# A two-layer attention and expert kernel: rank-one updates added by DMA, experts split beside the first half

## The reference

```python
x = x + xattn(c, layernorm(x), ...)        # 8 heads of 128; keys and values from c and x together
x = x + ffn(layernorm(x), W1, W2, scale)   # hidden width 1024, with rank-one updates per batch
x = x + attention(layernorm(x), c, c)      # one head of width 256
x = x + experts(layernorm(x), ...)         # 8 experts of inner width 256, mixed by a routing weight
```

```python
lt = x[:, 1:17]                            # 16 rows of the normed batch
even, odd = lt[:, ::2], lt[:, 1::2]
m1 = (even[:, :4, :, None] * odd[:, :4, None, :]).reshape(B, 1024, 256)
m2 = (even[:, 4:, :, None] * odd[:, 4:, None, :]).reshape(B, 256, 1024)
h = gelu(x @ W1.T + scale * einsum('bsd,bhd->bsh', x, m1) + b1)
out = h @ W2.T + scale * einsum('bsh,boh->bso', h, m2) + b2
```

## Time and profile before

| | us |
|---|---|
| median of 3 runs | 1989.06 (1987.77 to 1990.6) |
| the profiled execution | 1991.09 |
| its span, first to last instruction | 1989.3 |
| TensorE, busy | 1927.2 (97%) |
| VectorE, busy | 1367.9 (69%) |
| ScalarE, busy | 1115.5 (56%) |
| GpSimd, busy | 407.1 (20%) |

### The profile page before, as it was taken

The page is one execution under the profiler, slowest core; times in us unless marked ns, Lnnn a source line. Parts: engine busy times, 40 slices in busy tenths (PEclk is TensorE's granted clock), DMA queues, the critical chain, the costliest instruction groups (busy, mean ns, idle before and its releaser), DMA issues.

```text
span 1989.3 us, 41475 instructions
## 1 busy us (share of the span) xinstructions
PE 1927.2 (97%) x14078; PEld 1803.2 (91%) x14078; DVE 1367.9 (69%) x3408; ACT 1115.5 (56%) x2334; POOL 407.1 (20%) x650
## 2 busy tenths in 40 slices
PE   7999999999999999999987899999999999999998
PEld 6788888888888888888886899999999999999998
DVE  7877776776777776776746566766666666766665
ACT  5655565555655565555655655554555555544553
POOL 2222222222222222222213511111111101111100
PEclk9999999999999999999999999999999999999999
DMA  4000000000000000000012200000000000000000
...
DMA packets 47211, 44.51 MB, mean 22 GB/s; under 512 B 6848, under 2 KB 45376, under 8 KB 47168
## 3 DMA queue, kind: packets, MB, share of 16 engines
...
## 4 chain that ended last, share of the span: by engine, by line
PE 83%; DVE 7%; ACT 5%; issue 3%; POOL 1%; SPq 1%; DMA 0%; DVEq 0%; ACTq 0%; POOLq 0%
PE ring L618 9%; PE ring L620 9%; PE ring L619 9%; PE ring L1820 7%; PE ring L1818 7%; PE ring L1819 7%; PE ring L671 4%; PE sim L1818 3%; PE sim L1819 3%; PE sim L1820 3%; PE sim L618 3%; PE sim L620 2%; PE sim L619 2%; PE ps_x L1818 2%; PE ps_x L1820 2%
## 5 line engine op out<-in xcount | busy, mean ns | idle before, releaser
L411 ACT ACTIVATE a_pr<-sim,a_nmax 128x512 f32<-128x512 f32 x256 | 174.5, 689 | 208.4 <-DVE a_nmax L537 208.3
L1818 PE MATMUL ring<-b_xch,b_weh 128*128 128x256 f32 x1024 | 289.5, 283 | 1.7 <-DVE b_act_e L1464 1.7
L1819 PE MATMUL ring<-b_xcl,b_weh 128*128 128x256 f32 x1024 | 285.7, 279 | 0.0
L1820 PE MATMUL ring<-b_xch,b_wel 128*128 128x256 f32 x1024 | 285.6, 279 | 0.0
L326 POOL TENSOR_SCALAR a_pr<-a_pr,a_rinv 128x512 f32<-128x512 f32 x256 | 183.1, 729 | 498.3 <-DVE a_rinv L547 495.4
L1818 PEld LDWEIGHTS ring<-b_xch,b_weh 128*128 128x128 f32 x1024 | 192.3, 188 | 1.9 <-DVE b_act_e L1464 1.9
L1819 PEld LDWEIGHTS ring<-b_xcl,b_weh 128*128 128x128 f32 x1024 | 193.0, 188 | 0.0
L1820 PEld LDWEIGHTS ring<-b_xch,b_wel 128*128 128x128 f32 x1024 | 192.1, 188 | 0.0
L1464 DVE TENSOR_TENSOR b_act_e<-b_act_e,ring 128x512 f32<-128x512 f32 x128 | 87.9, 687 | 116.7 <-PE ring L1820 102.4
L528 DVE TENSOR_TENSOR a_ptl<-ring,a_pth 128x512 fp32r<-128x512 f32 x256 | 163.9, 682 | 3.1 <-ACT a_pth L401 2.0
L515 DVE SCALAR_TENSOR_TENSOR a_ktl<-ring,a_bkv_s,a_kth 128x512 fp32r<-128x512 f32 x128 | 95.3, 744 | 102.1 <-ACT a_kth L391 102.1
...
## 6 DMA issues: line engine op xcount, KB each, us to landing
...
b_up<-b_ev SPq DMA_DIRECT2D x256, 1.0 KB
...
```

The costliest lines, as they stand in the source:

```text
L411: nc.scalar.activation(pr[:, h % 2, t, :], sim[t][:], ACT.Exp, bias=nmax[:, h % 2, t:t + 1], accum_out=rsum[:, h % 2, t:t + 1]).then_inc(e ...
L1818: nc.tensor.matmul(out, lh, rh, start=(n == 0), stop=False)
L1819: nc.tensor.matmul(out, lh, rl, start=False, stop=False)
L1820: last = nc.tensor.matmul(out, ll, rh, start=False, stop=(n == len(parts) - 1 and not more))
```

## The change

1. The rank-one updates are written into the weights. 8 ScalarE instructions of 128x256 for W1 and 8 for W2 (`update`; GpSimd does them for batches 0 and 1) write scale x even x odd into `w1_raw` and `w2_raw`. One DMA for each matrix (`weights_added`, from GpSimd's queue, with `accum_op=ADD`) adds W1 or W2 from DRAM to it. Then the sum is split again for each batch: 8 copies of 128x512 (`weight_high`) on ScalarE, 8 subtractions on VectorE (`weight_low`; GpSimd does most for batches 0 and 1).
2. The 16 rows are normalised apart: SyncE loads 32 rows of x1 two batches ahead (`rows_load`), `rows_stats`, `rows_rstd` and `rows_apply` norm them, `rows_in_order` turns those for W2, and SyncE writes them to DRAM (`rows_between`) and reads them back: the even ones broadcast to all partitions (`even_b`, 1 MB), the odd ones with one number per element (`odd_raw`, 2 loads); `odd_scaled` multiplies these by the scale.
3. `z_fill`, the `up1` matmul in `h_fill`, `g_fill`, `y_update` and what served them are gone, and `y_fill` has 256 columns. `bias_x1`, `bias_x2` and the row shifts move from GpSimd to VectorE. The chain's steps, routing and weights of experts stand in another order within the body; `third_residual` writes a buffer of its own, `x3_s`.
4. The experts' weights are split in batches 1 to 8 of the first half, one expert in each (`spare`): SyncE loads 768 KB, ScalarE makes three copies and VectorE three subtractions, and SyncE writes both halves to DRAM (`expert_halves`). `experts_in` loads both, 12.6 MB in all, and the second half splits no expert. Batch 0 no longer loads or splits W1 and W2.
5. Batch 14 of the first half (`ahead`) makes the weights of the second half's batch 0, and batch 15 (`beside`) those of batch 1. The first half's loop is now batch 0, 1 to 8, 9 to 13, 14, 15; the second half's is bodies 1 to 13, 14, 15, 16.

```diff
         body(sections["first"], 0, False, True)
-        with eng.Fori(1, B - 1) as b:
+        with eng.Fori(1, 1 + SPARE) as b:
+            body(Order(loop_names, loop_first - F, sections["first"], F, b), b, True, True, True)
+        with eng.Fori(1 + SPARE, B - 2) as b:
             body(Order(loop_names, loop_first - F, sections["first"], F, b), b, True, True)
+        body(Order(loop_names, tail_first - F, Order(loop_names, 0)), B - 2, True, True)
...
-        with eng.Fori(2, B - 1) as t:
-            body(t, True, True, False)
+        with eng.Fori(1, B - 2) as t:
+            body(t, True, True, True)
+        body(B - 2, True, True, False)
         body(B - 1, True, False, False)
         body(B, False, False, False)
...
-        def updates_of(n):
-            take(ev_lo, n + 1)
...
+        def rows_load(n):
+            sp.dma_start(first_rows[:], x1_r[n]).then_inc(rows_in, 16)
+        def rows_spread(n):
+            take(rows_ready, n + 1)
+            sp.dma_start(z_t[n, 0:2 * NL], first_rows[1:1 + 2 * NL, :]).then_inc(rows_out, 16)
+            sp.dma_start(z_two[n, 1, NL:2 * NL], first_rows[2 + 2 * NL:2 + 4 * NL:2, :]).then_inc(rows_out, 16)
+            take(rows_turned, n + 1)
+            sp.dma_start(z_two[n, 0, NL:2 * NL], turned_rows[1 + 2 * NL:1 + 4 * NL:2, :]).then_inc(rows_out, 16)
+            take(rows_out, n * 48 + 48)
+            if not (isinstance(n, int) and n == 0):
+                take(w_made["2"], n * 4)
+            sp.dma_start(even_b[:], z_two[n, 0].unsqueeze(0).to_broadcast([P, 2 * NL, D])).then_inc(spread_in, 16)
+            for c in range(DC):
+                sp.dma_start(odd_raw[:, c, :], z_two[n, 1][:, c * P:(c + 1) * P].rearrange("r p -> p r"),
+                             allow_slow_non_contiguous=True).then_inc(spread_in, 16)
...
-            for j, w in enumerate((Wg[e], Wu[e], Wd[e])):
-                sp.dma_start(we_raw[e][:, j], w.rearrange("(c p) d -> p c d", p=P)).then_inc(expert_in[e], 16)
+            for part, tile in enumerate((weh[e], wel[e])):
+                sp.dma_start(f32(tile[:]).rearrange("p j c d -> p (j c d)"), kept[part, e]).then_inc(expert_in[e], 16)
+        def spare(h, b):
+            if h == 0:
+                take(split_out, b * 32)
+                sp.dma_start(w1_raw[:].rearrange("p c n -> p (c n)")[:, 0:3 * DC * D], We[b - 1]).then_inc(split_in, 16)
+            else:
+                take(split_lo, b * 3)
+                for part, tile in enumerate((w1h, w1l)):
+                    sp.dma_start(kept[part, b - 1], all_thirds(tile)).then_inc(split_out, 16)
...
+        def odd_scaled(n):
+            take(spread_in, n * 48 + 48)
+            nc.gpsimd.tensor_scalar(odd[:], odd_raw[:], lscale, 1.0, ALU.mult, ALU.mult).then_inc(odd_ready, 1)
+            take(odd_ready, n + 1)
...
+        def update(n, w, q):
+            if n > 0:
+                take(full["H", 3] if w == "1" else y_full, n if w == "1" else n * ST)
+            for k in range(2):
+                part, row, by = rank_one(w, q, k)
+                last = nc.gpsimd.tensor_scalar(part, row, by, 1.0, ALU.mult, ALU.mult)
+            last.then_inc(w_made[w], 1)
...
+        def weights_added(n, w):
+            take(w_made[w], n * 4 + 4)
+            if w == "1":
+                dst, src = w1_raw[:].rearrange("p c n -> p (c n)"), W1T.rearrange("p c n -> p (c n)")
+            else:
+                dst, src = w2_raw[:], W2T.rearrange("p c d -> p (c d)")
+            pool.dma_start(dst, src, accum_op=ALU.add, max_dma_last_dim=HC * W2ROW * 2).then_inc(w_in[w], 16)
...
+        def update(n, w, q):
+            act.wait_ge(odd_ready, n + 1)
+            if w == "1":
+                act.wait_ge(full["H", 3], n)
+            else:
+                act.wait_ge(y_full, n * ST)
+            for k in range(2):
+                part, row, by = rank_one(w, q, k)
+                last = nc.scalar.activation(part, row, ACT.Copy, scale=by)
+            last.then_inc(w_made[w], 1)
+        def weight_high(n, w, q):
+            act.wait_ge(w_in[w], n * 16 + 16)
+            raw, high, _ = (w_piece(w, q, tile) for tile in W[w])
+            nc.scalar.activation(high, raw, ACT.Copy).then_inc(w_hi[w], 1)
...
+        def spare(h, b):
+            if h < 3:
+                act.wait_ge(split_in, b * 16)
+                nc.scalar.activation(third(w1h, h), third(w1_raw, h), ACT.Copy).then_inc(split_hi, 1)
...
                 silu(i, 1)
-                routing_exps(i)
                 hidden_high(i, 1)
                 if chain:
                     gelu_high(t, 0)
                     gelu_high(t, 1)
-                for e in warm_in(1) if warm else ():
-                    for j in range(3):
-                        expert_high(e, j)
                 if chain:
                     gelu_high(t, 2)
                     gelu_high(t, 3)
+                routing_exps(i)
 
                 silu(i, 2)
                 if chain:
                     context_high(t)
                 hidden_high(i, 2)
-                for e in warm_in(2) if warm else ():
-                    for j in range(3):
-                        expert_high(e, j)
-                if chain:
-                    for k in range(ST):
-                        g_high(t, k)
-                    gt_copy(t)
+                if more:
+                    for q in range(4):
+                        update(t + 1, "1", q)
 
                 silu(i, 3)
                 hidden_high(i, 3)
-                for e in warm_in(3) if warm else ():
-                    for j in range(3):
-                        expert_high(e, j)
+                if chain:
+                    copy_high(t, "V", hh[:, V, 0:S])
+                if more:
+                    update(t + 1, "2", 0)
+                if chain:
+                    copy_high(t, "B", xth[:])
+                if more:
+                    update(t + 1, "2", 1)
 
                 silu(i, 4)
-                if chain:
-                    copy_high(t, "B", xth[:])
-                    copy_high(t, "V", hh[:, V, 0:S])
                 hidden_high(i, 4)
-                for e in warm_in(4) if warm else ():
-                    for j in range(3):
-                        expert_high(e, j)
                 if chain:
                     queries_high(t)
-                    row_shift_sums(t)
+                if more:
+                    update(t + 1, "2", 2)
+                    update(t + 1, "2", 3)
 
                 silu(i, 5)
+                if chain:
+                    softmax_exps(t)
+                hidden_high(i, 5)
                 if more:
-                    even_high(t + 1)
-                hidden_high(i, 5)
-                if chain:
-                    softmax_exps(t)
+                    weight_high(t + 1, "1", 0)
+                    weight_high(t + 1, "1", 1)
+                if chain:
+                    copy_high(t, "T", hh[:, PT, 0:S])
                 silu(i, 6)
...
+        def weight_low(n, w, q):
+            dve.wait_ge(w_hi[w], n * 4 + q + 1)
+            raw, high, low = (w_piece(w, q, tile) for tile in W[w])
+            nc.vector.tensor_tensor(low, raw, f32(high), ALU.subtract).then_inc(w_lo[w], 1)
...
+        def row_shifts(n):
+            dve.wait_ge(ln_ready["B"], n + 1)
+            for k in range(ST):
+                last = nc.vector.scalar_tensor_tensor(pr[:, k, :], ln[:, k, :], 1.0, v_b[:], ALU.mult, ALU.mult,
+                                                      accum_out=row_sum[:, k:k + 1])
+            last.then_inc(shift_in, 1)
+            take(shift_in, n + 1)
+            nc.vector.tensor_scalar(row_shift[:], row_sum[:], shift[:, 0:1], None, ALU.add).then_inc(shift_ready, 1)
...
-        def z_fill(n):
-            pe.wait_ge(od_ready, n + 1)
-            for c in range(DC):
-                for k, x in enumerate((xth, xtl)):
-                    last = nc.tensor.matmul(bank(n, "Z")[:, 0:S], od[:, c, :], x[:, c, :],
-                                            start=(c == 0 and k == 0), stop=(c == DC - 1 and k == 1))
-            last.then_inc(full["Z"], 1)
...
         def h_fill(t, n):
             cd = halves(bank(t, ("H", n)))
             for k in range(2):
                 cols = slice((2 * n + k) * P, (2 * n + k + 1) * P)
-                product(cd[:, k, :], range(DC), lambda c: w1h[:, c, cols], lambda c: w1l[:, c, cols],
-                        lambda c: xth[:, c, :], lambda c: xtl[:, c, :], more=True)
-                last = nc.tensor.matmul(cd[:, k, :], up1[:, n, k * P:(k + 1) * P], zm[:], start=False, stop=True)
+                last = product(cd[:, k, :], range(DC), lambda c: w1h[:, c, cols], lambda c: w1l[:, c, cols],
+                               lambda c: xth[:, c, :], lambda c: xtl[:, c, :])
             last.then_inc(full["H", n], 1)
 
...
         def y_fill(t, k):
             q = slice(k * P, (k + 1) * P)
-            product(bank(t, f"Y{k}")[:, 0:W2ROW], range(HC), lambda c: hh[:, c, q], lambda c: hl[:, c, q],
```

(14 more changed lines are left out.)

676 lines of the change are left out of this document (345 added, 331 removed).

## The result

The changed kernel takes 1970.82 us (median of 4 runs, 1969.19 to 1973.13) against 1989.83: ratio 0.9907, 95% interval 0.9894 to 0.9920. The profiled execution has a span of 1969.4 us. It is faster, as forecast, but by 19 us instead of 60, and the time lies 1 us above the stated range.

The account below looks back on a forecast made before the run. TensorE, busy 97% of the span and holding 83% of the chain, was taken as the bound. Terms summed to 60.4 us off the profiled 1991.1, giving 1930.7, and 1929 us for the median; range 1914 to 1970.

Parts of the forecast that it names:

- steady bodies, t = 2 to 15: Second half's 14 steady bodies: 2.7 us saved less 0.3 of new waits, 2.4 us each, 33.6 us in all.
- the second half's first body: No expert is split there, so it falls from 67.28 to 53.7 us: 13.6 us gained, bounds 10 to 14.
- batch 0: First half: split of W1 and W2 leaves, shortening the key-half wait, with clock and idle time: 4.5 us gained (2 to 5).
- batches 1 to 8: First half: three added copies on ScalarE and three subtractions on VectorE per batch fit into idle time: 0 us.
- batch 14: First half: 16 updates and two waits for small loads added on GpSimd: 1 us lost, bounds 0 to 3.
- batch 15: Where the halves meet: the 5.6 us wait goes, plus clock and removed matmuls: 9.7 us gained (7 to 12).
- the size of the new waits in a steady body: TensorE waiting on evictions behind added ScalarE and VectorE work: 0.3 us a body taken, bounds 0 and 2.
- The removed matmuls: Steady body: fewer matmuls and transposes and a narrower `y_fill` on TensorE save 2.2 us, all on the path.
- signs of being wrong: A wait on W2's low part before `y_fill`, first-half batches 1 to 8 over 64.0 us, or `h_fill` waiting for W1 copies.
- Rival B: VectorE or ScalarE slack used up: fills wait behind weight copies, 1.0 to 1.3 us a body remain; 1954 us, chance 0.21.
- Rival C: Accumulating DMA lands late by a little, up to 4 us a body: 1944 to 1989 us, chance 0.12.
- The single numbers: `odd_raw` loaded as 2048 single numbers might be slow and start updates late in every body; no price given.

Follow-up runs that it names:

- experiment 2: Changed kernel without the accumulating DMAs of batches 2 to 15, ScalarE's and VectorE's weights' work kept: 1956.76 us.
- 5: Changed kernel with W1's accumulating DMA on GpSimd held until x1 has landed, the root of norm B put first: 1959.08 us.
- 1: Changed kernel without the weights' work (updates, accumulating DMAs, copies, subtractions) for batches 2 to 15: 1951.48 us.
- 13: As 5, with the queries' high half (ScalarE) and low half (VectorE) ahead of expert 4's hidden halves: 1951.45 us.
- 8: Changed kernel with the biases of x1 and x2 added on GpSimd again: 1968.53 us.
- 9: As 5, with both biases on GpSimd again, that of x2 behind the root of norm A: 1977.06 us.
- 3: Changed kernel with W1's accumulating DMA held until x1 has landed, the root of norm B queued behind that wait: 2010.88 us.
- 4: Changed kernel with expert 4's hidden step and the queries' low half ahead of row sums and norm A's statistics on VectorE: 1972.11 us.
- 6: As 4 on the changed kernel, with the scores' maxima also ahead of norm A's statistics on VectorE: 1983.37 us.
- 10: The edits of 4 and 5 together on the changed kernel: 1969.93 us.
- 11: As 5, with GpSimd's odd rows and weight updates in batch 14 spread over slots 4 to 6: 1958.81 us.
- 12: As 11, with the bias of x2 behind the transposed probabilities and batch 14's second row statistics a slot later on VectorE: 1961.51 us.
- 14: As 13 with 11's spreading of batch 14, and the second set of rows loaded ahead of the even rows: 1952.32 us.
- 15: As 14, with ScalarE's four W1 copies for the second half's first batch all in slot 7 of batch 14: 1948.92 us.

## Why the prediction was wrong, step by step

| term | forecast | measured | |
|---|---|---|---|
| steady bodies, t = 2 to 15 | 33.6 | 3.7 | routing matmul of t = 1 to that of t = 15: 785.4 and 781.7 us |
| the second half's first body | 13.6 | 9.3 | |
| batch 0 | 4.5 | 5.6 | |
| batches 1 to 8 | 0 | -0.5 | |
| batch 14 | -1 | -4.5 | |
| batch 15 | 9.7 | 6.4 | |
| sum | 60.4 | 20.0 | the spans differ by 19.9 |

**The step that failed is the size of the new waits in a steady body.** The removed matmuls came as worked out, 2.1 us and not 2.2, and the norm's wait of 0.5 (0.7 with the matmul in front of it) went. But the new waits measure 2.7 us against the 0.3 taken, above the 2 that I gave as their upper bound. The runs divide them: 0.74 for the load of x1 beside W1's accumulating DMA (experiment 2; 0.68 came back in 5), 0.62 for the instructions of the weights' work on ScalarE and VectorE (1 against 2), and 1.3 for the new order with the moved steps (1 against the matmuls' own 53.33). Of these last two, 0.44 is ScalarE's making expert 4's hidden half ahead of the queries (13 against 5). The other 0.9 or more of the last part is not settled; that the biases stand on VectorE is not its cause, since on GpSimd they cost more (8 and 9 against 5). None of the signs of being wrong that I had named appeared: no wait stands in front of a product for a half of W1 or W2, and batches 1 to 8 take 64.0 us. The distance between routing products, 56.0 us and not 53.7, was the one sign that showed it.

I argued that VectorE had 9 us of idle time left in a body and was therefore nearer to zero. It had more, 12 us, and this did not help: the share of idle time says nothing of a hand-off whose predecessors stand in line. Rival B came nearest, by its list of hand-offs in series. It had 1.0 to 1.3 us of the gain left in a body and 1954 us; with the collision out of the way (5) 0.8 us are left and the kernel takes 1959. What B left out is the collision. That the measured 1971 us lies within the 1944 to 1989 of rival C is chance, as the next paragraph shows.

**Rival C looked at the accumulating DMAs and asked the wrong question.** I asked whether they land in time for their own reader. They do: 9.3 and 8.7 us, within the 8 to 11 taken, and in no steady body does ScalarE wait for them. I did not ask what else is in flight beside them. Before, the DMA engines were 5% busy in a body and x1's load had them to itself; W1's DMA now starts one microsecond ahead of it. That the two would fall close together could have been read from the order of the steps and the trace of before; what it costs could not, for the trace of before has no accumulating DMA. The same step failed for the first body, where x1's load held the norm up by 1.6 us and TensorE by 2.3, at a granted clock of 0.97 over the body; with 5 this body takes 54.8 us at 1.00, 12.5 of the forecast 13.6. The experts' halves, 12.6 MB, were in time.

**Batch 14** was taken at 1 us within 0 to 3; it lost 4.5. With the same batch 14 the profiles are of two kinds: 66.6 to 66.8 us, with the granted clock at 0.90 to 0.95 and then 0.84 to 0.88 in the stretches 961 to 969 and 969 to 977 (the changed kernel, experiments 3 and 4), and 64.9 to 65.2 with it at 1.00 (1, 2, 5, 6, 8, 9, 10 and 13). So 1.6 us go with the clock, and why it falls in some executions and not in others is open. The rest has waits in line: GpSimd 8.3 us for the odd rows with a division behind it, VectorE 1.5 us for a load, and, where these are taken away, ScalarE 4.2 us for W1's DMA. I had named GpSimd's. Taking one or two away moved the idle time to the third and made the batch longer (11, 12, 14: 66.3, 66.9 and 65.7 us against 65.0), and all three gave 1.6 us of the batch (15 against 13) and 2.5 us of the time. About 1.3 us over the old batch stay; whether they are the bare amount of work no run shows.

GpSimd's wait and TensorE's behind it, in the changed kernel:

```profile
963.30 0.28 POOL L1096 TENSOR_SCALAR b_odd<-b_odd_raw,b_factors 128x16 f32<-128x16 f32 x1 [8.30 <-DMA b_odd_raw<-rows_between]
...
966.66 0.63 PE L701 MATMUL ring<-ident,a_pr 128*128 128x128 f32 x4 [1.86 <-POOL a_pr L344]
```

**Right by their own steps:** batch 0 (the wait of 2.6 us for `a_ktl` ahead of the scores is gone, none is over 0.4 now, and the clock is 1.00 in the stretch), batches 1 to 8 (the six added instructions cost 0.06 us a batch), and the wait of 5.6 us for `b_up` in batch 15, which is gone. There, new waits of 2.8 and 1.2 us for low halves (against 1.9 and 0.6) ate a part; no run tells their cause. An update measures 0.50 us where I took 0.46, 0.6 us more for ScalarE in a body.

**The single numbers.** One load of `b_odd_raw`, 4 KB, takes 5.4 us, as long as the 1 MB of even rows beside it, and the packets under 512 bytes rose from 6848 to 39072, by 2014 a batch for 2048 numbers, with the old small loads gone from the same count. The rule of the Trainium skill ("DMA: Bandwidth & Descriptors", section "Rules for kernel authors"), one descriptor for each element of a strided last dimension, agrees with this count. In the steady body GpSimd waits for it for some 14 us with nothing behind that TensorE waits for, and TensorE's list shows no trace of it; in batch 14 the same wait was in the way.

```profile
DMA packets 101974, 119.24 MB, mean 61 GB/s; under 512 B 39072, under 2 KB 87072, under 8 KB 101920
...
b_odd_raw<-rows_between SPq DMA_DIRECT2D x32, 4.0 KB, 5.4
```
